# Stage Moe7 scores and chooses experts by parts, has no shared blocks on GpSimd and seven shared blocks in front; some reordering in Ternary and Ttt

## What is computed

```
# stage Ternary (L2_ffn)
w_ternary = where(w > d, 1, where(w < -d, -1, 0))      # d = 0.7 * mean(|w|)
x = x + (layernorm(x) @ (w_ternary * alpha).T + bias)
# stage Ttt (L3_attn)
q, k, v = split(layernorm(x) @ qkv_w + qkv_b, 3)       # q, k normalised per head of 8
for _ in range(2): theta = theta - 0.1 * newton_schulz(grad of mean((swish(k@gate) * (k@val)) @ proj - v)**2)
x = x + (swish(q@gate) * (q@val)) @ proj @ proj_w + proj_b
# stage Moe7 (L3_ffn), the last
logits = xf @ router_w.T                               # 7 experts
top_vals, top_idx = top_k(logits, 2); top_w = softmax(top_vals)
routed_out = (silu(xf @ w_gate[e]) * (xf @ w_up[e])) @ w_down[e]       # D=128, hidden 512
x = x + sum over the two experts of top_w * routed_out + swiglu_shared(xf)
```

## Time and profile before

| | |
|---|---|
| runs | 1680.59, 1687.51, 1689.58 us, median 1687.51 |
| profiled execution | 1679.48 us, its span 1677.4 us, mean granted TensorE clock 0.886 |
| busy, share of the span | PE 75%, DVE 59%, ACT 40%, POOL 39% |
| the chain that ended last | PE 51%, DVE 13%, POOL 12%, issue 10%, DMA 6%, ACT 5% |
| Ternary ends, Ttt begins | about 1100 us |
| Moe7 begins | about 1464 us |

### The profile page before, as it was taken

The page is one execution under the profiler, slowest core; times in us unless marked ns, Lnnn a source line. Parts: engine busy times, 40 slices in busy tenths (PEclk is TensorE's granted clock), DMA queues, the critical chain, the costliest instruction groups (busy, mean ns, idle before and its releaser), DMA issues.

```text
span 1677.4 us, 23947 instructions
## 1 busy us (share of the span) xinstructions
PE 1264.7 (75%) x8790; PEld 761.1 (45%) x8790; DVE 982.8 (59%) x1746; ACT 669.4 (40%) x1253; POOL 659.1 (39%) x647
## 2 busy tenths in 40 slices
PE   5467677531684668788778489979988998994997
PEld 2123332320453224434357234445555556683997
DVE  7899899860111988878453554366545554551333
ACT  3754233120353347767722335643323323231432
POOL 1288878377576430000034200025512440054443
PEclk9679899756897769989979699989999999996999
DMA  6257568011332422211001322150000000001112
GB/s 221 104 178 265 209 232 276 18 50 51 88 94 83 163 95 68 64 47 29 9 27 30 123 92 61 38 217 4 1 0 1 0 1 1 1 25 46 48 39 92
DMA packets 75445, 133.80 MB, mean 80 GB/s; under 512 B 12723, under 2 KB 39670, under 8 KB 74688
## 3 DMA queue, kind: packets, MB, share of 16 engines
q1 hardware_dynamic: 66400, 115.97, 20.9%
q0 software_dynamic: 8064, 13.87, 2.5%
q10 hardware_dynamic: 864, 2.43, 0.4%
HBM read 96.22 MB, written 38.38 MB: 80 GB/s over the span
## 4 chain that ended last, share of the span: by engine, by line
PE 51%; DVE 13%; POOL 12%; issue 10%; DMA 6%; ACT 5%; SPq 3%; POOLq 0%; DVEq 0%; ACTq 0%
PE ps L3662 6%; PE ps L1752 5%; POOL sb_arena L1018 5%; POOL xe L1116 3%; PE ps L3674 3%; PE ps L2119 2%; PE ps L644 2%; DVE sb_arena L1818 2%; ACT sb_arena L2066 2%; PE ps L2102 2%; PE ps L2973 2%; PE ps L2970 2%; PE ps L2962 1%; PE ps L2964 1%; DMA sb_arena<-xe 1%
## 5 line engine op out<-in xcount | busy, mean ns | idle before, releaser
L1818 DVE TENSOR_REDUCE sb_arena<-ps 128x2 f32<-128x1024 f32 (+2 forms) x192 | 211.1, 1130 | 60.7 <-PE ps L2347 34.2
L2066 ACT ACTIVATE sb_arena<-ps 128x512 f32<-128x512 f32 (+1 forms) x320 | 160.3, 554 | 58.6 <-PE ps L2119 54.9
L644 PE MATMUL ps<-sb_arena,sb_const 128*128 128x512 f32 x256 | 136.2, 677 | 27.9 <-DVE sb_arena L837 27.9
L831 DVE TENSOR_TENSOR_SCAN sb_arena<-ps,sb_arena 128x1024 f32<-128x1024 f32 x64 | 144.9, 2279 | 4.9 <-ACT ps L926 3.9
L1850 POOL CAST sb_arena<-sb_arena 128x8 bf16<-128x8 f32 (+2 forms) x32 | 6.5, 204 | 293.1 <-DVE sb_arena L1818 149.9
L1752 PE MATMUL ps<-sb_arena 128*32 128x256 f32 (+3 forms) x1856 | 117.6, 361 | 0.4 <-ACT sb_arena L2300 0.2
L3808 DVE TENSOR_TENSOR sb_arena<-sb_arena,ps 128x512 f32<-128x512 f32 x56 | 38.4, 687 | 111.8 <-PE ps L3662 111.8
L1116 POOL DMA_INDIRECT xe<-sb_arena x80 | 79.9, 999 | 51.0 <-issue 30.5
L644 PEld LDWEIGHTS ps<-sb_arena,sb_const 128*128 128x128 f32 x256 | 56.1, 221 | 93.5 <-issue 53.5
L1018 POOL TENSOR_TENSOR sb_arena<-sb_Wreg,sb_arena 128x1024 f32<-128x1024 f32 x32 | 79.0, 2490 | 40.3 <-DMA sb_arena<-bcrows 32.1
L3514 POOL TENSOR_TENSOR sb_arena<-sb_arena 128x512 f32<-128x512 f32 x32 | 40.7, 1270 | 137.2 <-DVE sb_arena L3192 137.2
(11 more groups left out here) (479 smaller groups left out, 2856.0 us busy)
## 6 DMA issues: line engine op xcount, KB each, us to landing
sb_arena<-bcrows SPq DMA_DIRECT2D x80, 512.0 KB, 6.4
xe<-sb_one SPq DMA_DIRECT2D x31, 260.0 KB, 8.9
sb_Wreg<-e0w SPq DMA_DIRECT2D x24, 256.0 KB, 7.2
sb_arena<-xe SPq DMA_DIRECT2D x16, 325.0 KB, 3.1
y<-sb_zero SPq DMA_DIRECT2D x20, 256.0 KB, 6.7
sb_arena<-y SPq DMA_DIRECT2D x4, 1024.0 KB, 9.1
sb_Wreg<-e1w SPq DMA_DIRECT2D x16, 256.0 KB, 2.7
sb_Wreg<-e3gu SPq DMA_DIRECT2D x1, 4096.0 KB, 12.5
```

Of the source, the lines that this page charges most:

```text
L644: t = e.matmul(k.b(self.Y + c), k.c("ident"), self.hc[i % 4][:, c * 512:(c + 1) * 512], start=False, stop=n == 15)
L831: e.tensor_tensor_scan(self.hh[i % 3], k.pair(2 * (i % 2)).rearrange("p c t -> p (c t)"), self.dB[i % 3], 0.0, MUL, ADD).then_inc(S.scan.s ...
L1818: e.tensor_reduce(dst, src, AX.X, MAX).then_inc(S.mxr.sem, 1)
L2066: e.activation(self.PT[s % 4][:, 2 * h:2 * h + 2, 0:n], bank[:, :, 0:n], ACT.Exp, scale=self.scale).then_inc(S.ex.sem, 1)
```

## The change

In **Ternary** the bias of chunk 3 goes from ahead of chunk 1's transposes to just ahead of chunk 3's matmuls. In **Ttt** PE projects tiles 0 to 3 ahead of chunk 1's transposes instead of behind them, and ACT copies the first keys ahead of value and query 3. In **Moe7** the scores of a chunk follow its transposes, into bank 4 (chunks 0 to 2) and bank 5 (chunk 3), each with a release of `lg`; ACT copies chunks 0 and 1 ahead of the last square root; DVE chooses for 12 tiles, then for 4; PE makes the counts ahead of every block; ACT does the Exp ahead of its copy of the rows (`xq`) and of every silu; the multiplies on POOL and the copies to `uc` are gone, all multiplies are DVE's and come after placing; seven shared blocks are in front and one is behind.

```diff
@@ Ternary.pe
         self.bias_pe(e, 2)
-        self.bias_pe(e, 3)
         self.f.chunk_pe(e, w, self.ln.wait_rows, 1)
...
         self.out_pe(e, w, 2)
+        self.bias_pe(e, 3)
         self.out_pe(e, w, 3)
@@ Ttt.pe
         self.f.chunk_pe(e, w, self.ln.wait_rows, 0)
-        self.f.chunk_pe(e, w, self.ln.wait_rows, 1)
         w.wait_ge(S.g_w, 16)
         w.wait_ge(self.before.S.fxa, 4)
         self.qkv_pe(e, w, range(0, 4))
+        self.f.chunk_pe(e, w, self.ln.wait_rows, 1)
         self.f.chunk_pe(e, w, self.ln.wait_rows, 2)
@@ Ttt.act
         self.root_act(e, w, 2)
-        self.value_act(e, w, 3)
-        self.query_act(e, 3)
         w.wait_ge(S.ktp, 1)
         e.copy(self.kT[:, 0:512], k.b(0)).then_inc(S.kT.sem, 1)
+        self.value_act(e, w, 3)
         self.root_act(e, w, 3)
+        self.query_act(e, 3)
@@ Moe7
-    BLK, NB, FRONT, EARLY = 256, 22, 6, 2
+    BLK, NB, FRONT = 256, 22, 7
+
+    PARTS = [(0, 12, 4), (12, 16, 5)]
@@ Moe7.pe
+    def scores_pe(self, e, w, c):
+
+        k = self.k
+        self.f.wait(w, c)
+        bank = k.b(self.PARTS[c // 3][2])
+        for i in range(4 * c, 4 * c + 4):
+            t = e.matmul(bank[:, i * 8:(i + 1) * 8], self.xnT[:, i * 128:(i + 1) * 128], k.s("rw3"), start=True, stop=True)
+        return t
+
...
-        self.f.pe(e, w, self.ln.wait_rows)
+        self.f.chunk_pe(e, w, self.ln.wait_rows, 0)
+        self.f.chunk_pe(e, w, self.ln.wait_rows, 1)
+        self.scores_pe(e, w, 0)
+        self.f.chunk_pe(e, w, self.ln.wait_rows, 2)
+        self.scores_pe(e, w, 1)
+        self.scores_pe(e, w, 2).then_inc(S.lg.sem, 1)
+        self.f.chunk_pe(e, w, self.ln.wait_rows, 3)
+        self.scores_pe(e, w, 3).then_inc(S.lg.sem, 1)
         w.all(self.before.ends)
-        lg = k.b(7)[:, 0:128]
...
+        self.count_pe(e, w)
         w.wait_ge(k.g_w["e3"], 32)
...
-            if v == 1:
-                self.count_pe(e, w)
@@ Moe7.choose_dve
-        w.wait_ge(S.lg, 1)
-        w.mark(e.tensor_copy(self.p, k.b(7)[:, 0:128]))
...
+        for x, (a, z, bank) in enumerate(self.PARTS):
+            w.wait_ge(S.lg, x + 1)
+            w.mark(e.tensor_copy(self.p[:, 8 * a:8 * z], k.b(bank)[:, 8 * a:8 * z]))
...
+            for i in range(a, z):
+                t = e.max(v8[:, i, :], p3[:, i, :])
@@ Moe7.dve
-        for v in range(self.EARLY):
-            self.home_dve(e, w, v)
-        for v in range(self.EARLY, last):
+        for v in range(last):
@@ Moe7.act
-            w.wait_ge(S.mu, n + 1)
-            e.copy(self.uc[y], k.b(2 * y + 1)).then_inc(S.uc.sem, 1)
...
+        self.ln.act(e, w, ready, (0, 1, 2))
+        self.f.chunk_act(e, w, 0)
+        self.f.chunk_act(e, w, 1)
+        self.ln.act(e, w, ready, (3,))
+        self.f.chunk_act(e, w, 2)
+        self.f.chunk_act(e, w, 3)
         w.all(self.before.ends)
+        w.wait_ge(S.shift, 1)
+        e.activation(self.d, self.d, ACT.Exp).then_inc(S.probs.sem, 1)
         self.ln.wait_rows(w, 3)
         e.copy(self.xq[1][:, :, 0:128], self.xn).then_inc(S.xq.sem, 1)
@@ Moe7.pool
-            e.tensor_tensor(self.h[v % 3][:, 2 * y:2 * y + 2, :], self.sg[y].rearrange("p (q t) -> p q t", q=2),
-                            self.uc[y].rearrange("p (q t) -> p q t", q=2), MUL).then_inc(S.hp.sem, 1)
```

More of the change, by code:

```diff
@@ L3562, in __init__ @@
         self.S = S = k.signals(
-            **chunk_signals(), lg=1, shift=1, probs=1, chosen=1, cnt=1, eid=1, iw=1, gu=NB, dn=NB, ids=2, wts=2, xq=1, scat=512,
-            **{f"load{i}": 16 * ((NB + 5 - i) // 6) for i in range(6)}, tr=NB, xT=NB, mg=60, mu=60, sg=60, uc=2 * self.EARLY, hp=2 * self.EARLY, h=60 - 2 * self.EARLY, o=30, oa=2 * NB, ox=8,
+            **chunk_signals(), lg=2, shift=1, probs=1, chosen=1, cnt=1, eid=1, iw=1, gu=NB, dn=NB, ids=2, wts=2, xq=1, scat=512,
+            **{f"load{i}": 16 * ((NB + 5 - i) // 6) for i in range(6)}, tr=NB, xT=NB, mg=60, mu=60, sg=60, h=60, o=30, oa=2 * NB, ox=8,
             **{f"row{i}": 32 * ((NB + 3 - i) // 4) for i in range(4)}, **{f"back{c}": 16 for c in range(4)}, fin=4, out=64)
@@ L3586, in __init__ @@
         self.xT = [A.take(256) for _ in range(3)]
-        self.sg, self.uc = [A.take(512) for _ in range(2)], [A.take(512) for _ in range(2)]
+        self.sg = [A.take(512) for _ in range(2)]
         self.h = [B.take(1024).rearrange("p (b t) -> p b t", b=4) for _ in range(3)]
@@ L3615, in wait_h @@
     def wait_h(self, w, n):
-        early = 2 * self.EARLY
-        w.wait_ge(*((self.S.hp, n + 1) if n < early else (self.S.h, n + 1 - early)))
+        w.wait_ge(self.S.h, n + 1)
     def wait_out(self, w, v):
@@ L3655, in up_pe @@
             src = self.xT[m % 3]
-        if 2 <= n < 2 + 2 * self.EARLY:
-            w.wait_ge(S.uc, n - 1)
-        elif n >= 2:
+        if n >= 2:
             self.wait_h(w, n - 2)
@@ L3718, in choose_dve @@
         v8, i8 = self.v8, self.i8
-        w.wait_ge(S.lg, 1)
-        w.mark(e.tensor_copy(self.p, k.b(7)[:, 0:128]))
[L3721 to L3730, removed]
+        for x, (a, z, bank) in enumerate(self.PARTS):
+            w.wait_ge(S.lg, x + 1)
+            w.mark(e.tensor_copy(self.p[:, 8 * a:8 * z], k.b(bank)[:, 8 * a:8 * z]))
+            w.own()
+            w.mark(e.tensor_copy(p3[:, a:z, 7], k.c("padneg").to_broadcast([128, z - a])))
+            w.own()
+            for i in range(a, z):
+                t = e.max(v8[:, i, :], p3[:, i, :])
+            w.mark(t)
+            w.own()
+            for i in range(a, z):
+                t = e.max_index(i8[:, i, :], v8[:, i, :], p3[:, i, :])
+            w.mark(t)
         w.own()
@@ L3836, in dve @@
         last = len(self.blocks)
-        for v in range(self.EARLY):
-            self.home_dve(e, w, v)
-        for v in range(self.EARLY, last):
+        for v in range(last):
             for n in (2 * v, 2 * v + 1):
                 self.mul_dve(e, w, n)
-            if v > self.EARLY and self.blocks[v - 1][0] == "s":
+            if v and self.blocks[v - 1][0] == "s":
                 self.home_dve(e, w, v - 1)
```

16 lines of the change are left out of this document (1 added, 15 removed).

## The result

Ten runs of the changed kernel have a median of **1670.61 us** (1663.07 to 1674.65), ten of the kernel before 1681.09 us (1676.10 to 1689.58). The ratio (taken from the single runs; the quotient of these two medians is 0.9938) is **0.9929**, 95% interval 0.9909 to 0.9949: 5.1 to 8.9 parts in a thousand less, 8.6 to 15.3 us. The profiled execution took 1669.69 us, its span is 1667.8 us at a mean granted clock of 0.886, 9.6 us under the span of before.

A forecast was written before the change was run, and what follows sets the result against it. Bound: the last stage's chain from scores through choosing and scatters to TensorE's first gathered rows. Terms -8.7 - 0.35 - 1.1 - 1.8 + 0.2, about -11.8 us, put the median at 1675.7 (range 1671 to 1681; with rivals 1668 to 1683).

The forecast's parts named there:

- Choosing chain: Last stage, from scores to row numbers on TensorE and VectorE: row numbers come 8.7 us earlier.
- The three operations: VectorE between counts' copy and row numbers: 1.11, 1.13 and 1.25 us long beside GpSimd's multiplies; removing those gains 2.7.
- The counts' copy: VectorE's copy of the counts in the last stage: starts at about 1474.8, 6.0 us earlier.
- Rival 1: Last stage: three VectorE operations stay long and scores run at half clock; gain 9.1 to 6.6, 1678.4 to 1680.9; chance 0.2.
- The cover: Seven shared blocks in front on TensorE finish before the gathered rows come, with 12.8 us of margin.
- block 0 costs twice, some 3.5 us more: First front block on TensorE at half clock after its new wait of about 4 us; lies inside the margin.
- Rival 4: TensorE stays at half clock through the front, blocks cost 10.5 us: slower, time 1696; chance 0.05, other unseen losses included.
- The end: Kernel end: one trailing shared block fewer gains 0.35 us, not 5.24, since the last addition waits for loads back.
- Rival 3: The seventh block gives its whole 5.24 us at the kernel's end; time 1670.8; chance 0.05.
- Ternary and Ttt: Reordered TensorE work at the boundary of these stages gains 1.1 us in Ternary and 1.8 in Ttt.
- ScalarE's order: Ttt: copying the keys ahead of value and query 3 loses 0.2 us (0 to 0.6).
- Rival 2: Ternary to Ttt boundary gives nothing because VectorE sets the pace; gain 9.0, time 1678.5; chance 0.07.

The follow-up runs named there:

- warmexp: The changed kernel plus an Exp of constants on ScalarE ahead of its wait for the shifted scores; 1662.56 us, one run.
- parts: The kernel before with only scores and choosing by parts and ScalarE's order of the chunk copies in the last stage; 1674.05 us, one run.
- front8: The changed kernel with all eight shared blocks in front and none behind the last rows; 1672.23 us, one run.
- poolmul: The changed kernel with three unused GpSimd multiplies of 128 x 512, operands in SBUF, beside VectorE's placing; 1664.69 us, one run.
- boundary: The kernel before with only the edits in Ternary and Ttt; 1675.64 us, ratio 0.9976 (0.9949 to 1.0003).

## Why the prediction was right, term by term

- **Time.** Forecast 1675.7 from a median of 1687.5, a ratio of 0.9930; measured 0.9929. The measured median of 1670.6 is 5.1 us lower, and 0.4 under the forecast's own range of 1671 to 1681 (the one with the rivals, 1668 to 1683, holds it), because ten runs of before have a median of 1681.1: the three shown lay 6.4 high. That the two ratios agree to one part in ten thousand is luck: the interval is 0.9909 to 0.9949, and the terms measured below add up to less than the forecast.
- **Choosing chain, -8.7: -7.7.** The three operations gave 2.76 (2.7 forecast), for the reason given. The counts' copy came 4.9 us earlier after the tile, not 6.0. About half of that miss is the first copy, which I had put at +0.45 (it is +0.94); the rest is the Exp, which I had taken as ready: its table load, 1.28 us, waits with it. VectorE's 0.79 for it are returned by warmexp.
- **Rival 1.** Its first half, that the three operations keep their length, is refuted. Its second, half clock during the scores, didn't come in the changed kernel's trace, where the clock fell 2.65 us after the last tile, but it did in parts, and cost the cast 1.0 us there.
- **The cover.** Margin 12.8 forecast, 13.0 found, with half clock at the start of the front as foreseen. The prediction's "block 0 costs twice, some 3.5 us more" is the price of its up passes alone (3.62); a whole block is 5.24. The first 32 passes in front cost 2.8 more. Rival 4 didn't come: blocks from 1484.26 on follow at 5.24. Its sum starts six blocks at 1481.5 where the cover starts them at 1480.3, so its time was 1.2 too long.
- **The end, -0.35: -0.34** in this pair; front8 shows that scatter and loads set it. Rival 3 is refuted.
- **Ternary and Ttt, -2.7 in all: -1.8.** At the second key addition 2.9 were gained, as summed (1.1 + 1.8). ScalarE's order took 0.34 back instead of 0.2, and the first forward matmuls at half clock 0.75, which I had not counted. Rival 2 is refuted.
- **Sum.** -11.8 forecast; the profiled pair has -9.1 without the 0.5 from stages that are unchanged, the interval of the ratio 8.6 to 15.3. Why the runs may gain more than this pair stays open. The old chain was 19.4 us in one execution and 22.4 in another, by TensorE's clock; the new one was never over 11.77 in six traces (poolmul apart), but in none of these did the clock fall early, and parts shows that scores by parts lose by that as well. How often each comes is not measured.
- **What I had not seen.** The parts are not a term of their own, as I had priced them: with counts and Exp behind the early blocks they gave 0 or 2.8 us, by which execution one compares with, and 4.05 with both moved. The sum held because the change also moves counts and Exp.

## What to carry to other kernels

When a chain is shortened at its head, look at every point further down where it joins another engine's queue: parts gave 0 us against before with the counts behind 24 matmuls, and 4.05 without. Compare such stretches only where TensorE's clock fell at the same point, or name the difference. An activation that needs another table should have a dummy of its function ahead of its wait, where the engine is idle anyway, since the load waits with it. Keep GpSimd off operations that read SBUF while VectorE has operations with two SBUF inputs on the path; three memsets cost nothing here.

## What the runs showed of the hardware

- The table load stands behind the semaphore wait of its activation: 1.28 us, at 1471.52 right after 3.94 us of idle, and at 1462.57 with a dummy ahead. The Trainium skill (ScalarE: Activation LUTs, "What ACT_TABLE_LOAD costs") gives 1283 ns for it; the rows agree.
- Three GpSimd multiplies of 128x512 took 3.15 us beside VectorE's operations and stretched those by 2.0 in all; three memsets of that size took 1.45 and stretched nothing.
- TensorE's clock differs between executions of the same rows: 32 score passes took 4.96 us in one and 6.83 in another, two forward passes 1.10 and 2.05. In twelve of the fourteen traces the granted clock fell to 0.50 between 1.9 and 2.9 us after the last normalised tile of Moe7, in the other two (boundary, parts) at its end. A chain that waits for such short matmuls inherits that.
